# Cross-attention on one core: maxima taken from pairs of banks, two banks for scores, and two tiles in four quads of a head added up on VectorE

## The chip, the cores and the metric

The kernel runs on one core of one Trainium2 chip. The metric is the device time of one execution in microseconds (us). A core has five engines that work side by side, each through its own queue in order: TensorE (PE in the profile; its weight loads are PEld), VectorE (DVE), ScalarE (ACT), GpSimd (POOL) and SyncE (SP), which here issues the DMAs. TensorE writes its results to PSUM, eight banks of 128 partitions by 512 fp32 numbers; VectorE and ScalarE read them from there.

## What is computed

A block of three layers on x of 512 tokens by 512, with a context of 8192 tokens by 384. The change touches the first, a cross-attention with 16 heads of width 32:

```python
q = (x @ Wq + bq).reshape(B, N, NUM_HEADS, HEAD_DIM)
k = (y @ Wk + bk).reshape(B, M, NUM_HEADS, HEAD_DIM)
v = (y @ Wv + bv).reshape(B, M, NUM_HEADS, HEAD_DIM)
scores = jnp.einsum('bnhd,bmhd->bhnm', q, k) * scale
attn = jax.nn.softmax(scores, axis=-1)
out = jnp.einsum('bhnm,bmhd->bnhd', attn, v).reshape(B, N, IMAGE_DIM)
h = jax.nn.relu(out @ W1 + b1)
return h @ W2 + b2
```

N is 512 queries, M 8192 keys. A local attention and a feed-forward layer with quantized weights follow; nothing in them changes.

## The kernel before

The first 343 us project keys and values (stage "project"); the attention runs from there to about 1115 us (stage "attend"); its MLP, the local attention and the feed-forward layer fill the rest.

The keys of a head are cut into 16 **quads** of 512 keys, each into four tiles of 128. The softmax takes two passes over the scores. The first pass needs the maximum of each query: with queries on the partitions, `pre_tile` (L1042) computes 128 queries by 512 keys into a bank of `pre_ps` with four matmuls of 32 columns, and VectorE's `tile_max` (L1297) reduces it to one number a query. This pass runs two quads (`AHEAD`) before the head that uses it, so it is mixed into the work of the head before. `head_max` (L1304) reduces the 16 numbers, `row` (L1066) turns them into a row of the stacked queries, and ScalarE's `copy_row` (L1231) puts it there. The second pass has keys on the partitions: `scores` (L1079) computes one tile of 128 keys by 512 queries into a bank of `s_ps`, ScalarE writes its exponential (L1261) to `prob`, which has four slots of a quad. From `prob` come `weighted` (L1092, four fp32 matmuls a quad, summed over the head in one bank) and the denominator: GpSimd adds up tiles 0 to 2 of a quad, or 0 and 1 (even quads from 2 on), over the head (`add_up`, L1435 and L1439); `add_to_denominator` (L1103) lets TensorE sum over the partitions the one or two tiles that are left, four matmuls of 128 columns a tile; `denominator` (L1119) closes the sum with GpSimd's three tiles behind quad 1 of the next head, `invert` (L1309) takes the reciprocal, `output` (L1130) and `scale_out` (L1316) write the head's result behind quad 5.

**PSUM.** Three banks hold scores (`S_BANKS`), three hold maxima tiles, the output and the row in turn (`PRE_BANKS`), one the weighted values, one the denominator. The scores of tile n are written when the exponential of the tile that had their bank is done (semaphore `p_ready`; `s_back` says how many tiles back that is: three but for a few at the end of a head and the start of the next, two for the last tile). A maxima tile waits for the reduction three turns back (`pre_read`).

**The order of TensorE** in a quad is written out by hand, and `head` follows it, with `weighted` of the quad before at the end:

```python
PE_ORDER = ((0,), 0, (1,), 1, "den", 2, (2,), 3, (3,))
```

A number in brackets is a maxima tile, a bare one a scores tile, "den" is `add_to_denominator` for the quad two before. The last head has no maxima to take for a next one; in it VectorE does GpSimd's part (`sum_tiles`, L1345 and L1349).

## Time and profile before

| | us |
|---|---|
| median of 3 runs | 1390.31 (1388.82 to 1392.01) |
| the profiled execution | 1390.34 |
| its span | 1388.6 |
| TensorE busy | 1339.1 (96%) |
| VectorE busy | 1121.1 (81%) |
| ScalarE busy | 806.0 (58%) |
| GpSimd busy | 778.2 (56%) |

The span is from the first instruction to the last on the core; the execution's own time is 1.7 us longer. Busy time is the union of an engine's instructions. Four matmuls of 32 columns each run beside each other and are shown as four rows with nearly the same start; a matmul's row of 0.4 us reaches over the start of the next group 0.22 us later, so what a group costs is read from start to start. "Idle before" in brackets is the time in which the engine did nothing ahead of a group, with what ended it.

### The profile page before, as it was taken

The numbers are of one execution on the slowest core, as the hardware profiler recorded it, in microseconds if no ns is written. First come the engines' busy times: TensorE is split into PE (matmuls) and PEld (weight loads), VectorE is DVE, ScalarE is ACT, GpSimd is POOL, SyncE is SP. The second block draws the span as 40 slices with busy tenths as digits, with TensorE's granted clock in tenths as the row PEclk, the third lists the DMA queues.
The fourth block names the chain that finished last, engine by engine and source line by source line (L and its number), as shares of the span: only waits on it lengthen the run. The fifth ranks groups of instructions, "written<-read, shape, count | busy, mean of one in ns | idle before, by whom it ended". The sixth has DMA issues, their size and how long they took to land. (4 is left out here: it accounts for less than half of the span.)

```text
span 1388.6 us, 40034 instructions
## 1 busy us (share of the span) xinstructions
PE 1339.1 (96%) x17126; PEld 706.7 (51%) x17126; DVE 1121.1 (81%) x1786; ACT 806.0 (58%) x1459; POOL 778.2 (56%) x320
## 2 busy tenths in 40 slices
PE   7999999998999999999999999999999998999998
PEld 4444444444655554555555555545554445566554
DVE  5778888887888888888888888888886854678895
ACT  4454444453777777776777777777777831254332
POOL 0321222222999988998998898899889000201121
PEclk9999999999999999999999999999999999999999
DMA  7667777786352122121212212121211030491000
GB/s 263 178 172 227 213 216 205 207 234 186 87 176 69 38 68 67 41 64 57 69 39 68 67 38 60 64 69 38 68 55 31 5 144 1 97 226 23 0 9 23
DMA packets 127800, 137.54 MB, mean 99 GB/s; under 512 B 44996, under 2 KB 108996, under 8 KB 125700
## 3 DMA queue, kind: packets, MB, share of 16 engines
q1 hardware_dynamic: 127622, 134.98, 34.4%
q8 instruction: 135, 2.21, 0.7%
q14 instruction: 43, 0.34, 0.1%
HBM read 75.70 MB, written 44.17 MB: 86 GB/s over the span
## 5 line engine op out<-in xcount | busy, mean ns | idle before, releaser
L1297 DVE TENSOR_REDUCE early<-attend_banks 128x1 f32<-128x512 f32 x952 | 612.2, 685 | 80.8 <-PE attend_banks L1042 75.6
L1261 ACT ACTIVATE attend_prob<-attend_banks 128x512 f32<-128x512 f32 x1024 | 535.9, 600 | 200.5 <-PE attend_banks L1079 198.3
L1439 POOL TENSOR_TENSOR early<-early,attend_prob 128x1024 f32<-128x1024 f32 x210 | 614.0, 2924 | 37.7 <-ACT attend_prob L1261 9.6
L1079 PE MATMUL attend_banks<-early,k_first 97*32 97x512 f16 x2560 | 258.9, 382 | 3.1 <-ACT attend_prob L1261 3.1
L1042 PE MATMUL attend_banks<-k_first,early 96*32 96x512 f16 x2272 | 233.2, 382 | 1.1 <-PEq L285 1.1
L1042 PE MATMUL attend_banks<-attend_k_rest,early 96*32 96x512 f16 x1536 | 155.9, 380 | 0.0
L1079 PE MATMUL attend_banks<-early,attend_k_rest 97*32 97x512 f16 x1536 | 152.4, 380 | 2.8 <-ACT attend_prob L1261 2.8
L1103 PE MATMUL attend_banks<-attend_prob,ones 128*32 128x128 f32 x3048 | 134.0, 272 | 3.7 <-DVE attend_recip L1309 3.7
L1092 PE MATMUL attend_banks<-attend_prob,wkv_area 128*32 128x512 f32 x1024 | 134.2, 592 | 0.0
L1092 PE MATMUL attend_banks<-attend_prob,attend_vh_odd 128*32 128x512 f32 x1024 | 133.1, 592 | 0.0
L503 POOL TENSOR_TENSOR project_w_whole<-project_grid,project_qscale 128x704 f32<-128x704 f32 x24 | 33.3, 1386 | 172.9 <-DVE project_grid L636 172.9
L1103 PEld LDWEIGHTS attend_banks<-attend_prob,ones 128*32 128x32 f32 x3048 | 94.9, 110 | 55.1 <-DVE attend_recip L1309 11.1
L1079 PEld LDWEIGHTS attend_banks<-early,k_first 97*32 97x32 f16 x2560 | 77.7, 97 | 84.9 <-ACT attend_prob L1261 54.9
L1042 PEld LDWEIGHTS attend_banks<-k_first,early 96*32 96x32 f16 x2272 | 69.7, 97 | 60.1 <-issue 35.5
L555 ACT ACTIVATE project_v<-project_v_ps 128x512 f32<-128x512 f32 x64 | 38.1, 597 | 91.3 <-PE project_v_ps L771 91.3
L497 POOL TENSOR_TENSOR project_qn<-early,project_qinv 128x704 f32<-128x704 f32 x24 | 37.9, 1581 | 87.5 <-issue 50.2
L539 ACT ACTIVATE early<-project_k_ps,project_bk 128x512 f32<-128x512 f32 x64 | 44.0, 687 | 63.2 <-PE project_k_ps L752 62.4
L769 PE MATMUL project_v_ps<-project_w_hi,project_yT_hi 128*128 128x512 f16 x192 | 73.6, 383 | 4.2 <-ACT project_v L555 4.2
L1079 PEld LDWEIGHTS attend_banks<-early,attend_k_rest 97*32 97x32 f16 x1536 | 45.5, 96 | 58.7 <-ACT attend_prob L1261 45.0
L752 PE MATMUL project_k_ps<-project_yT_hi,project_w_hi 128*128 128x512 f16 x192 | 72.5, 379 | 1.9 <-ACT project_q_hi L574 1.4
L770 PE MATMUL project_v_ps<-project_w_lo,project_yT_hi 128*128 128x512 f16 x192 | 73.5, 383 | 0.0
L771 PE MATMUL project_v_ps<-project_w_hi,project_yT_lo 128*128 128x512 f16 x192 | 73.4, 382 | 0.0
(217 smaller groups left out, 1839.2 us busy)
## 6 DMA issues: line engine op xcount, KB each, us to landing
v_scratch<-project_v SPq DMA_DIRECT2D x16, 1024.0 KB, 9.0
early<-in_ctx_dram SPq DMA_DIRECT2D x16, 768.0 KB, 6.2
k_first<-k_scratch SPq DMA_DIRECT2D x36, 256.0 KB, 3.5
k_scratch<-project_k_hi SPq DMA_DIRECT2D x64, 128.0 KB, 2.9
k_scratch<-project_k_lo SPq DMA_DIRECT2D x64, 128.0 KB, 3.1
attend_vh_odd<-v_scratch SPq DMA_DIRECT2D x8, 1024.0 KB, 5.0
wkv_area<-v_scratch SPq DMA_DIRECT2D x7, 1024.0 KB, 4.8
attend_k_rest<-k_scratch SPq DMA_DIRECT2D x24, 256.0 KB, 3.4
```

What stands on the lines that cost most here:

```text
L539: nc.scalar.activation(kf[:, g % 2], k_ps[:, g % 2], ACT.Identity, bias=bk[:, g:g + 1], scale=1.0 / WSCALE).then_inc(kf_ready, 1)
L752: last = nc.tensor.matmul(k_ps[:, g % 2], (w_lo if p == 2 else w_hi)[:, 0, k, cols], (yT_lo if p == 1 else yT_hi)[:, u, k], start=(k, p) = ...
L769: nc.tensor.matmul(v_ps[:, t % 2], yT_hi[:, u, k, cols], w_hi[:, 1, k], start=k == 0, stop=False)
L770: nc.tensor.matmul(v_ps[:, t % 2], yT_hi[:, u, k, cols], w_lo[:, 1, k], start=False, stop=False)
L771: last = nc.tensor.matmul(v_ps[:, t % 2], yT_lo[:, u, k, cols], w_hi[:, 1, k], start=False, stop=k == CK - 1)
L1042: last = nc.tensor.matmul(pre_ps[c * HD:(c + 1) * HD, bank, :], q_stack[0:KROWS, h, queries], keys_at(s, part * BLK, (part + 1) * BLK)[0:K ...
L1079: last = nc.tensor.matmul(s_ps[c * HD:(c + 1) * HD, s_bank[n], :], key_rows[:, c * HD:(c + 1) * HD], q_stack[0:KROWS + 1, h, :], start=Tru ...
L1092: last = nc.tensor.matmul(pv_ps[t * HD:(t + 1) * HD, :], vh[s][:, BT * q + t, :], prob[:, q % PSLOTS, t, :], start=q == 0, stop=q == QUADS ...
L1103: last = nc.tensor.matmul(den_ps[t * HD:(t + 1) * HD, 0:P], ones[:], prob[:, q % PSLOTS, n, t * P:(t + 1) * P], start=q == 0 and n == summ ...
L1261: nc.scalar.activation(prob[:, q % PSLOTS, t, :], s_ps[:, s_bank[BT * q + t]], ACT.Exp, scale=SCALE).then_inc(p_ready, 1)
L1297: nc.vector.tensor_reduce(part_max[:, s, j, part:part + 1], pre_ps[:, bank], AX.X, ALU.max).then_inc(pre_read, 1)
L1439: nc.gpsimd.tensor_tensor(sums, sums, prob[:, q % PSLOTS, 0:n], ALU.add).then_inc(pool_summed, 1)
```

## The change

- `S_BANKS` goes from three to two, and `s_back` is two for every tile: scores n wait for the exponential of tile n-2. `PE_ORDER` stays.
- `PRE_BANKS` goes from three to four, used as two pairs of neighbouring banks. Maxima tiles 0 and 1 of a quad fill one pair, 2 and 3 the other; `pre_ready` is raised once a pair, and `pair_max` reduces both banks in one instruction (2 x 512 columns to 2 numbers). The wait of TensorE (`pre_read`) stands ahead of the first tile of a pair, for the pair two turns back. The output and the row each take a turn with the first bank of a pair; so behind either of them the pairs of the following quads change sides.
- In quads 2, 6, 10 and 14 (`TWO_AT`) of all heads but the last, `add_two` lets VectorE add the two tiles that GpSimd leaves (fp32, 128 x 512, SBUF to SBUF) into `two_tiles`. It stands in VectorE's queue between the two pairs of the next quad. TensorE's `add_to_denominator` for these quads waits for it (`two_added`) and takes four matmuls in place of eight. `add_two` waits for the four exponentials of the quad, and for TensorE to have read `two_tiles` last.
- The banks that the MLP uses early are numbered anew; there are five, as before.

The diff, without hunks that only rename:

```diff
@@ -58,8 +58,8 @@
 PSLOTS = 4
 POOL_TILES = 3
 DVE_TILES = 2
-S_BANKS = 3
-PRE_BANKS = 3
+S_BANKS = 2
+PRE_BANKS = 4
 TILE_RING = 8
 PE_ORDER = ((0,), 0, (1,), 1, "den", 2, (2,), 3, (3,))
 CH = 4
...
@@ -863,6 +863,8 @@
             sum_pool = piece([2, POOL_TILES * T])
             recip = sb("recip", [P, P])
             o_out = sb("o_out", [P, 2, P])
+            two_tiles = sb("two_tiles", [P, T])
+            two_added = sem("two_added")
             banks = ps("banks", [P, S_BANKS + PRE_BANKS + 2, T])
             s_ps = banks[:, 0:S_BANKS]
...
@@ -907,20 +909,27 @@
             OUTPUT_AT, ROW_AT = 5, QUADS - 2
+            PAIRS, ALL_PAIRS = TILES // 2, ALL_TILES // 2
             turns_of_head = []
             for q in range(QUADS):
-                turns_of_head += [(q, j) for j in range(TT)]
+                turns_of_head += [(q, 0), (q, 1)]
                 turns_of_head += ["output"] if q == OUTPUT_AT else ["row"] if q == ROW_AT else []
-            assert len(turns_of_head) % PRE_BANKS == 0
+            assert len(turns_of_head) % 2 == 0
             turn_of = {turn: n for n, turn in enumerate(turns_of_head)}
-            def tiles_until(n):
+            def bank_of(n):
+
+                return n % 2 * 2
+
+            def pairs_until(n):
                 return n + 1 if n < 0 else sum(turn not in ("output", "row") for turn in turns_of_head[:n + 1])
-
-            s_bank = [n % S_BANKS for n in range(TILES - 4)] + [0, 1, 2, 1]
-            s_back = [next(d for d in range(1, TILES) if s_bank[n - d] == s_bank[n]) for n in range(TILES)]
+            s_bank = [n % S_BANKS for n in range(TILES)]
+            s_back = [S_BANKS] * TILES
+
+
+            TWO_AT = (2, 6, 10, 14)
             def keys_at(s, lo, hi):
...
@@ -942,7 +951,7 @@
                 return DVE_TILES if q < LAST_SUMMED else 0
-            OUT_BANK = S_BANKS + turn_of["output"] % PRE_BANKS
+            OUT_BANK = S_BANKS + bank_of(turn_of["output"])
             h_bank = [b for b in range(S_BANKS, S_BANKS + PRE_BANKS) if b != OUT_BANK] + list(range(S_BANKS))
             EARLY_M = len(h_bank)
             h_bank += [PV_BANK, DEN_BANK, OUT_BANK]
...
@@ -1041,23 +1050,25 @@
                         queries = slice(j * P + c * HD, j * P + (c + 1) * HD)
                         last = nc.tensor.matmul(pre_ps[c * HD:(c + 1) * HD, bank, :], q_stack[0:KROWS, h, queries],
                                                 keys_at(s, part * BLK, (part + 1) * BLK)[0:KROWS], start=True, stop=True)
-                    last.then_inc(pre_ready, 1)
+                    if j % 2:
+                        last.then_inc(pre_ready, 1)
                 def pre(i, s, q, j):
                     h = 2 * i + s
                     s_of, part = (1 - s, q + AHEAD) if q < QUADS - AHEAD else (s, q + AHEAD - QUADS)
                     h_of = h + 1 if q < QUADS - AHEAD else h + 2
-                    n = turn_of[(q, j)]
+                    n = turn_of[(q, j // 2)]
                     if j == 0 and part % (QUADS // CH) == 0:
                         pe.wait_ge(k_in[s_of][part * CH // QUADS], 32 * (h_of // 2 + s_of))
-                    wait(pe, pre_read, TILES * h + tiles_until(n - PRE_BANKS))
-                    if n - PRE_BANKS == turn_of["output"]:
-                        wait(pe, o_scaled, h)
-                    if n - PRE_BANKS == turn_of["row"]:
-                        pe.wait_ge(row_set, h + 2)
-                    pre_tile(n % PRE_BANKS, h_of, s_of, part, j)
+                    if j % 2 == 0:
+                        wait(pe, pre_read, PAIRS * h + pairs_until(n - 2))
+                        if n - 2 == turn_of["output"]:
+                            wait(pe, o_scaled, h)
+                        if n - 2 == turn_of["row"]:
+                            pe.wait_ge(row_set, h + 2)
+                    pre_tile(bank_of(n) + j % 2, h_of, s_of, part, j)
                 def row(h, s, bank):
...
@@ -1098,10 +1109,14 @@
                     h = 2 * i + s
                     if q == 0:
                         wait(pe, recip_ready, h)
-                    for n in range(summed_tiles(h, q), BT):
+                    two = h < H - 1 and q in TWO_AT
+                    if two:
+                        pe.wait_ge(two_added, len(TWO_AT) * h + TWO_AT.index(q) + 1)
+                    for n in range(summed_tiles(h, q) + two, BT):
+                        tile = two_tiles if two else prob[:, q % PSLOTS, n]
                         for t in range(TT):
                             last = nc.tensor.matmul(den_ps[t * HD:(t + 1) * HD, 0:P], ones[:],
-                                                    prob[:, q % PSLOTS, n, t * P:(t + 1) * P],
+                                                    tile[:, t * P:(t + 1) * P],
                                                     start=q == 0 and n == summed_tiles(h, q), stop=False)
                     last.then_inc(den_added, 1)
...
@@ -1131,10 +1146,9 @@
                                                 pv_sum[:, s, t * P:(t + 1) * P], start=True, stop=True)
                     last.then_inc(o_ready, 1)
-                def tiles_read(h, n):
-
-                    tiles = TILES * h + tiles_until(n)
-                    return min(tiles, ALL_TILES) if isinstance(tiles, int) else tiles
+                def pairs_read(h, n):
+
+                    return min(PAIRS * h + pairs_until(n), ALL_PAIRS)
                 def head(i, s, first, last):
...
@@ -1160,12 +1174,12 @@
                             denominator(*before)
                         if q == OUTPUT_AT and not first:
                             n = turn_of["output"]
-                            pe.wait_ge(pre_read, tiles_read(h, n - PRE_BANKS))
-                            output(*before, n % PRE_BANKS)
+                            pe.wait_ge(pre_read, pairs_read(h, n - 2))
+                            output(*before, bank_of(n))
                         if q == ROW_AT and last >= 1:
                             n = turn_of["row"]
-                            pe.wait_ge(pre_read, tiles_read(h, n - PRE_BANKS))
-                            row(h + 1, 1 - s, n % PRE_BANKS)
+                            pe.wait_ge(pre_read, pairs_read(h, n - 2))
+                            row(h + 1, 1 - s, bank_of(n))
                 pe.wait_ge(fold_in, 16)
                 pe.wait_ge(ones_row, 16)
...
@@ -1291,15 +1305,24 @@
             @block.vector
             def _(dve):
-                def tile_max(s, part, j, tile, bank):
-
-                    dve.wait_ge(pre_ready, tile + 1)
-                    nc.vector.tensor_reduce(part_max[:, s, j, part:part + 1], pre_ps[:, bank], AX.X,
+                def pair_max(s, part, j, pair, bank):
+
+                    dve.wait_ge(pre_ready, pair + 1)
+                    nc.vector.tensor_reduce(part_max[:, s, 2 * j:2 * j + 2, part], pre_ps[:, bank:bank + 2], AX.X,
                                             ALU.max).then_inc(pre_read, 1)
+                def add_two(i, s, q):
+
+                    n = len(TWO_AT) * (2 * i + s) + TWO_AT.index(q)
+                    dve.wait_ge(p_ready, BT * (quad_no(i, s, q) + 1))
+                    if n:
+                        dve.wait_ge(den_added, quad_no(i, s, q) - 1 if q == TWO_AT[0] else quad_no(i, s, q - 4) + 1)
+                    nc.vector.tensor_tensor(two_tiles[:], prob[:, q % PSLOTS, BT - 2], prob[:, q % PSLOTS, BT - 1],
+                                            ALU.add).then_inc(two_added, 1)
+
                 def head_max(h, s):
-                    dve.wait_ge(pre_read, TILES * h - TT * AHEAD)
+                    dve.wait_ge(pre_read, PAIRS * h - TT * AHEAD // 2)
                     wait(dve, row_ready, h - 1)
                     nc.vector.tensor_reduce(neg_max[:, s], part_max[:, s], AX.X, ALU.max,
                                             negate=True).then_inc(max_ready, 1)
...
@@ -1378,9 +1401,12 @@
                             scale_out(*before, out_bank)
                         if last >= (1 if q < QUADS - AHEAD else 2):
                             s_of, part = (1 - s, q + AHEAD) if q < QUADS - AHEAD else (s, q + AHEAD - QUADS)
-                            for j in range(TT):
-                                tile_max(s_of, part, j, TILES * h + TT * q + j,
-                                         turn_of[(q, j)] % PRE_BANKS)
+                            for j in range(2):
+                                pair_max(s_of, part, j, PAIRS * h + 2 * q + j, bank_of(turn_of[(q, j)]))
+                                if j == 0 and q - 1 in TWO_AT:
+                                    add_two(i, s, q - 1)
+                        elif q - 1 in TWO_AT and last > 0:
+                            add_two(i, s, q - 1)
                         if q == QUADS - AHEAD - 1 and last >= 1:
                             head_max(h + 1, 1 - s)
                         if last == 0:

```

## Rows read from the trace of the kernel before

**Rows 1.** The page: busy times of the engines, and the exponentials.
```profile
PE 1339.1 (96%) x17126; PEld 706.7 (51%) x17126; DVE 1121.1 (81%) x1786; ACT 806.0 (58%) x1459; POOL 778.2 (56%) x320
...
L1261 ACT ACTIVATE attend_prob<-attend_banks 128x512 f32<-128x512 f32 x1024 | 535.9, 600 | 200.5 <-PE attend_banks L1079 198.3
```

**Rows 2.** Busy time by stretch (columns: us, each engine's busy us, clock, DMA), 351 to 1066.
```profile
351.00:1066.00 715.00, 708.39 (x12616) 375.60 (x12608) 622.49 (x983) 507.06 (x969) 653.03 (x222) 1.00 0.21 63
```

**Rows 3.** The waits (total us, times, longest), 351 to 1066.
```profile
ACT attend_prob L1261 <- PE attend_banks L1079: 190.5, 207, 1.4
PEld attend_banks L1079 <- ACT attend_prob L1261: 82.7, 288, 0.8
```

**Rows 4.** Order of time (start, us, engine; [idle before]), a quad with one denominator tile.
```profile
705.02 0.40 PE L1042 MATMUL attend_banks<-k_first,early 96*32 96x512 f16 x4
...
705.23 0.40 PE L1079 MATMUL attend_banks<-early,attend_k_rest 97*32 97x512 f16 x4
...
705.46 2.60 DVE L1297 TENSOR_REDUCE early<-attend_banks 128x1 f32<-128x512 f32 x4 [0.23 <-PE attend_banks L1042]
...
705.76 2.07 ACT L1261 ACTIVATE attend_prob<-attend_banks 128x512 f32<-128x512 f32 x4 [0.95 <-PE attend_banks L1079]
...
705.89 0.40 PE L1103 MATMUL attend_banks<-attend_prob,ones 128*32 128x128 f32 x8
...
706.11 0.40 PE L1079 MATMUL attend_banks<-early,attend_k_rest 97*32 97x512 f16 x4
...
706.40 0.10 PEld L1079 LDWEIGHTS attend_banks<-early,attend_k_rest 97*32 97x32 f16 x4 [0.18 <-ACT attend_prob L1261]
...
706.55 0.40 PE L1079 MATMUL attend_banks<-early,attend_k_rest 97*32 97x512 f16 x4
...
708.06 0.40 PE L1079 MATMUL attend_banks<-early,attend_k_rest 97*32 97x512 f16 x4
```

**Rows 5.** Order of time, maxima 3 of quad 5 and maxima 0 of quad 6.
```profile
700.67 0.40 PE L1042 MATMUL attend_banks<-k_first,early 96*32 96x512 f16 x4
...
701.97 0.40 PE L1042 MATMUL attend_banks<-k_first,early 96*32 96x512 f16 x4
```

**Rows 6.** Order of time, scores and exponentials of the last quad of a head.
```profile
728.93 0.59 PE L1079 MATMUL attend_banks<-early,attend_k_rest 97*32 97x512 f16 x4
...
729.73 1.58 ACT L1261 ACTIVATE attend_prob<-attend_banks 128x512 f32<-128x512 f32 x3
...
730.87 0.40 PE L1079 MATMUL attend_banks<-early,attend_k_rest 97*32 97x512 f16 x4 [0.26 <-ACT attend_prob L1261]
...
732.39 0.39 PE L1079 MATMUL attend_banks<-early,k_first 97*32 97x512 f16 x4
```

**Rows 7.** The reciprocals of 397 to 738.9 us, and scores 0 and 3 of one quad 2.
```profile
L1309 DVE RECIPROCAL attend_recip<-attend_banks x7: 957/958/959, 397.5 to 690.1; 128x128 f32<-128x128 f32 x7
...
397.51 0.39 PE L1079 MATMUL attend_banks<-early,k_first 97*32 97x512 f16 x4
...
399.24 0.40 PE L1079 MATMUL attend_banks<-early,k_first 97*32 97x512 f16 x4
```

**Rows 8.** VectorE: groups by line, order of time, and line 1349 (ns min/median/max).
```profile
L616 DVE TENSOR_REDUCE project_amax<-early 128x44 f32<-128x704 f32 x24 | 21.1, 878 | 0.2 <-DMA early<-in_L_ffn_w_gate_dram 0.2
...
725.75 0.22 DVE L1304 TENSOR_REDUCE early<-early 128x4 f16<-128x64 f32 x1
...
L1349 DVE TENSOR_TENSOR early<-early,attend_prob x12: 1214/1220/1227, 1079.6 to 1106.4; 128x1024 f32<-128x1024 f32 x12
```

**Rows 9.** Order of time, scores 0 and 1 of two quads of the last head.
```profile
1083.28 0.60 PE L1079 MATMUL attend_banks<-early,attend_k_rest 97*32 97x512 f16 x8
...
1085.54 0.60 PE L1079 MATMUL attend_banks<-early,attend_k_rest 97*32 97x512 f16 x8
```

**Rows 10.** Busy time by stretch, after the attention (columns as in rows 2).
```profile
1162.00:1166.00 4.00, 2.67 (x23) 2.24 (x21) 2.48 (x7) 0.98 (x2) 0.00 (x0) 1.00 0.00 0
1166.00:1170.00 4.00, 2.05 (x10) 1.12 (x11) 2.30 (x4) 1.30 (x3) 0.00 (x0) 0.88 0.02 4
```

More of the change, by code:

```diff
@@ L1200, in _ @@
                 pe.wait_ge(o_scaled, H - 1)
-                output(LASTPAIR, 1, turn_of["output"] % PRE_BANKS)
+                output(LASTPAIR, 1, bank_of(turn_of["output"]))
                 hidden(1, range(DK - 1))
@@ L1265, in head @@
                         if q == ROW_AT and last >= 1:
-                            copy_row(h + 1, turn_of["row"] % PRE_BANKS)
+                            copy_row(h + 1, bank_of(turn_of["row"]))
                         if last == 0 and q in O_HIGH_AT:
@@ L1331, in split_weights @@
                                                    op0=ALU.mult, op1=ALU.subtract).then_inc(mlp_split, 1)
-                out_bank = turn_of["output"] % PRE_BANKS
+                out_bank = bank_of(turn_of["output"])
                 SPLIT_AT = (2, 4, 5, 7, 8, 10)
```

## The prediction

> **What bounds the kernel now.** I read the page first. TensorE is busy 96% of the span, VectorE 81%, ScalarE and GpSimd under 60% [rows 1]. Two thirds of the span are the attention of 16 heads, so I took the busy times of 351 to 1066 us, where 15 heads with maxima for the next head run: TensorE shows 708.4 of 715 us at a granted clock of 1.00, VectorE 622, GpSimd 653, ScalarE 507 [rows 2]. Matmul busy time overlaps itself, so I checked it against the order of time. A head is 16 quads, and a quad of TensorE is: maxima tile 0, scores 0, maxima 1, scores 1, sum of the denominator, scores 2, maxima 2, scores 3, maxima 3, weighted values. Groups of four follow each other every 0.22 us without a gap: maxima 0 at 705.02, scores 0 at 705.23, the denominator at 705.89, scores 2 at 706.11, and after maxima 2 scores 3 at 706.55 [rows 4]. A quad with one denominator tile takes 2.83 us (scores 0 at 705.23, the next at 708.06), one with two 3.05 us (maxima 0 at 701.97 to 705.02) [rows 4, 5]. TensorE bounds these heads by its order of work alone; ScalarE waits for it 190.5 us [rows 3]. The other wait in the list speaks of how near ScalarE is: weight loads of scores wait for ScalarE 82.7 us, 288 times [rows 3]. That wait costs nothing now, because it ends before the array is free: the load of scores 3 is let go at 706.40, its matmul has its turn at 706.55 [rows 4]. This is the place that the change touches.
>
> **Part 1, scores get two banks instead of three.** Scores n may be written when the exponential of tile n-3 is done now, of tile n-2 after; with that, scores 3 waits for exponential 1, and scores 2 for exponential 0. The chain is all in rows. Scores 0 starts at 705.23, its exponential at 705.76: 0.53. From that start to the release of a waiting load: 706.40 - 705.76 = 0.64 to 0.65. Exponentials follow each other every 0.49 us ((1.58 - 0.60) / 2) [rows 1, 4, 6]. So scores 2 can start 0.53 + 0.64 = 1.17 us after scores 0, and scores 3 at 0.53 + 0.49 + 0.64 = 1.66; take 1.65. Today scores 2 starts 0.88 after scores 0 (706.11) and scores 3 1.32 (706.55) in a quad with one denominator tile, 0.22 more in one with two. There is one place where the kernel of before has just this wait: in the last quad of each head scores 3 has the bank of scores 1. There the exponentials start at 729.73, so the second at 730.22, and scores 3 starts at 730.87, 0.65 later, weight load and matmul together, after an idle array [rows 6]. So nothing else is in the release, and nothing hides it: TensorE's queue is in order, and behind the wait stand maxima 2, maxima 3 and the weighted values. From scores 3 to the next scores 0 it is 708.06 - 706.55 = 1.51 as now, 0.01 more after an idle array. New quad: 1.65 + 1.52 = 3.17 us, whether it has one denominator tile or two.
> Per head: 7 quads with one tile (the odd ones but the last) +0.34 each = 2.4; 7 with two (0, 4, 6, ... 14) +0.12 each = 0.8. Quad 2 waits already for the reciprocal between scores 1 and 2: 397.51 to 399.24 = 1.73 from scores 0 to 3 [rows 7], over 1.65, so +0.0. Quad 15 pays its wait already, with an exponential that starts late behind the copy of the row of maxima: 3.46 us (728.93 to 732.39) [rows 6]; new 3.17, so -0.3. Sum 2.9 us.
>
> **Part 2, maxima in pairs.** A reduction of 704 columns takes 0.88 us, one of 64 columns 0.22: 1.03 ns for a column, so one over two banks 0.88 + 0.33 = 1.21 us; the upper bound is two single ones, 2.60 / 2 = 1.30 [rows 4, 8]. I take 1.20, since one instruction pays its start once. VectorE then has 2.4 us in a quad instead of 2.6. It wasn't the bound (its row has 0.23 of idle ended by TensorE [rows 4]), so this gains nothing. What it costs: a pair of banks comes free only when both tiles are read, and the next pair but one needs it. In a plain quad that is a whole quad later, with 0.6 us or more to spare. After the output (behind quad 5) and after the row (behind quad 14) the pairs change sides: maxima 0 of the next quad need the pair that maxima 2 and 3 of this quad wrote. From maxima 3 to the next maxima 0 it is 701.97 - 700.67 = 1.30 us now [rows 5], with output or row in between (0.22 each). New: reduction 0.44 after the matmuls (705.02 to 705.46 [rows 4]), 1.20 long, 0.05 for the release (an exponential's 0.65 less its 0.60): 1.69. So +0.39 twice a head, 0.8 us. The bounds are 0 (the read is hidden) and 0.5 (1.30 long). The bank of the output or the row itself is wanted by the second pair of the next quad, some 1.6 us after its first, time enough for one scaling or copy.
> By the Trainium skill, Perfetto Trace Analysis, section Optimizing Scalar/DVE Operations, grouping helps an engine that is saturated, and an engine that isn't but makes bubbles on another should have its instructions broken up. By the first half the pairs would free 0.2 us a quad; the trace shows VectorE waiting for TensorE (0.23 [rows 4]), so the second half is the one that applies here, with these 0.8 us.
>
> **Part 3, VectorE adds two tiles in four quads.** Sums of 128x1024 take 1.22 us here; with 512 columns less at 1.03 ns it is 0.69 [rows 8]. Four of them stand between the pairs of quads 3, 7, 11 and 15, which then hold 2.4 + 0.69 = 3.1 us of VectorE in 3.17, and the second pair ends 0.1 or 0.2 us late, with 0.6 to spare. VectorE waits there for exponential 3 of the quad before, which has ended before pair 0 of this quad is read. Behind it is queued only pair 1. TensorE wants the sum in the denominator step one quad later. On TensorE it takes away 16 matmuls in four of the quads with two tiles: 0.22 us each (705.89 to 706.11 [rows 4]), 60 quads in all, 13.2 us. But the step stands between scores 1 and scores 2, and scores 2 then waits for exponential 0: it would start at 1.17 with or without it. So the gain on the path is nil; the 13.2 us turn into waiting. Bounds: -13.2 (no such wait) and 0.
>
> **The last head** has no maxima; its quads take 1085.54 - 1083.28 = 2.26 us [rows 9]: by the chain above scores 3 starts 1.17 after scores 0 already, so 1.09 is left to the next scores 0. New: 1.65 + 1.09 = 2.74, 16 x 0.48 = +7.7 us. The MLP behind it has five early banks, as before: nothing.
>
> **Sum.** 15 x (2.9 + 0.8) = 55.5, less 0.4 for head 0, which has no output: 55.1; with 7.7 it is 63 us. On the profiled execution's 1390.34 us (span 1388.6, the median of the runs 1390.31, the same) that is 1453. As a check of the counting: 7 reciprocals mark six heads from 397.5 to 690.1, 48.77 us each [rows 7]; my quads of before (7 x 2.83, 7 x 3.05, 3.24, 3.46) with output, row and the closing sum of three denominator tiles (0.22 + 0.22 + 0.66) make 49.0.
>
> **Rivals.**
> Scores are not held back (not slower, or faster): if exponential 0 lets go of its bank within 0.88 us of scores 0, the third bank was spare, the 13.2 us of part 3 count in full and part 2 costs 11 at most: 1388, or 1377 if the read of a pair also hides. It decides below 0.88; the rows have 1.17 at each scores 3, and the last quads a real idle array. 4 in 100.
> The wait is longer than a release: a matmul after an idle array starts later by its weight load (0.10, the load at 706.40 [rows 4]). Then +0.1 in each of 256 quads, 1480; against it stands the start at 730.87 of load and matmul together. Half of it, 1467, is in my range. 6 in 100 for beyond 1474.
> VectorE becomes the bound: if the add next to GpSimd's sums takes twice as long (1.4), quads 3, 7, 11, 15 hold 3.8 us of VectorE against 3.17, and 0.6 of lateness meets 0.6 of spare. It would have to last longer still; at +0.5 in each of 60 quads, 1484. GpSimd, busy 653 of 715 us now [rows 2], gets 8% more time for the same sums. 2 in 100.
> TensorE's clock falls. It is at 2.4 GHz all through the heads, and stretches with gaps keep it (2.67 busy us of 4 at 1.00), while after one with 2.05 of 4 at 0.88 it has fallen [rows 10]. The new heads work 2.82 us of 3.17, the last one 2.2 of 2.74. Were it to fall, nearly each 0.22 would be 0.44: +2 us in 256 quads, 1900. 1 in 100. The Trainium skill (TensorE: Matmul & The Clock Gate, Part 1) has the same two states, set by how busy the array has been; by its rule the clock stays as well.
>
> **Numbers.** My forecast, slower by 3.5 to 6%, holds 87 in 100: the chain is pinned to some 0.05 us a quad (13 us), and pairs to 0.1 us at two places. Range 1438 to 1474. A measurement of this kernel can tell some 0.2%, 2.8 us, from no change. Faster by more 0.03, within 0.02, slower 0.95.
>
> **What would show it.** Quads of 3.17 us from scores 0 to scores 0, alike with one and with two denominator tiles; TensorE idle in front of scores 2 and scores 3, ended by the exponential; reductions of 1024 columns at 1.2 us; 2808 denominator matmuls instead of 3048 with no time to show for it; idle of 0.4 us in front of maxima 0 of quads 6 and 15, ended by VectorE. Quads of 2.9 us, or scores 2 starting 0.9 us after scores 0, would make the forecast wrong.

## The result, and the profile after

The changed kernel takes 1462.61 us (median of 4 runs, 1461.80 to 1464.76) against 1390.84 us for the kernel before: a ratio of 1.0519, 95% interval 1.0506 to 1.0532. It is 71.8 us slower. The forecast was 1453 us (1438 to 1474), 63 us slower.

| | before | after |
|---|---|---|
| median | 1390.84 | 1462.61 |
| span of the profiled execution | 1388.6 | 1461.5 |
| TensorE busy | 1339.1 | 1378.0 |
| VectorE busy | 1121.1 | 1122.6 |
| ScalarE busy | 806.0 | 827.0 |

The busy time of the stretch in which 15 heads take maxima for the next, 351 to 1130 us, answers to [rows 2]. The columns are those of [rows 2].

```profile
351.00:1130.00 779.00, 744.37 (x12136) 298.92 (x12132) 623.51 (x571) 524.91 (x967) 653.65 (x221) 1.00 0.20 58
```

TensorE is idle 35 us of 779 here, against 7 of 715, at the same granted clock of 1.00 (2.4 GHz). VectorE and GpSimd are busy for the same time as before (623.5 and 653.7 us, against 622.5 and 653.0) in a longer stretch. The waits of this stretch answer to [rows 3]:

```profile
ACT attend_prob L1275 <- PE attend_banks L1090: 232.4, 221, 1.7
PEld attend_banks L1090 <- ACT attend_prob L1275: 217.3, 633, 0.7
DVE early L1311 <- PE attend_banks L1051: 150.7, 382, 1.0
POOL early L1465 <- ACT attend_prob L1275: 69.8, 103, 1.3
```

The wait of the scores' weight loads (L1090 is L1079 of before) for ScalarE has grown from 82.7 us, 288 times, to 217.3 us, 633 times. ScalarE and VectorE wait more for TensorE, too: all of them stand in the one loop of scores, exponential and bank, and each of them has gaps in it. In order of time, one quad (it answers to [rows 4]):

```profile
702.85 0.39 PE L1090 MATMUL attend_banks<-early,k_first 97*32 97x512 f16 x4
...
703.37 2.19 ACT L1275 ACTIVATE attend_prob<-attend_banks 128x512 f32<-128x512 f32 x4 [0.99 <-PE attend_banks L1090]
703.50 0.39 PE L1118 MATMUL attend_banks<-attend_two_tiles,ones 128*32 128x128 f32 x8
703.51 1.23 DVE L1311 TENSOR_REDUCE early<-attend_banks 128x2 f32<-128x1024 f32 x1 [0.23 <-PE attend_banks L1051]
704.02 0.10 PEld L1090 LDWEIGHTS attend_banks<-early,k_first 97*32 97x32 f16 x4 [0.40 <-ACT attend_prob L1275]
704.02 0.40 PE L1090 MATMUL attend_banks<-early,k_first 97*32 97x512 f16 x4
...
704.51 0.40 PE L1090 MATMUL attend_banks<-early,k_first 97*32 97x512 f16 x4
...
706.03 0.39 PE L1090 MATMUL attend_banks<-early,k_first 97*32 97x512 f16 x4
```

Scores 0 start at 702.85, scores 2 at 704.02, scores 3 at 704.51, the next scores 0 at 706.03. That is 1.17, 1.66 and 3.18 us after scores 0; the forecast had 1.17, 1.65 and 3.17. Weight load and matmul of scores 2 start together at 704.02, 0.65 after the exponential of 703.37. The following quad, with an ordinary denominator tile, takes 3.19 (706.03 to the scores 0 of 709.22). Behind the row of maxima the new stall of the pairs is seen:

```profile
711.11 0.39 PE L1051 MATMUL attend_banks<-k_first,early 96*32 96x512 f16 x4
...
711.55 1.23 DVE L1311 TENSOR_REDUCE early<-attend_banks 128x2 f32<-128x1024 f32 x1 [0.45 <-PE attend_banks L1051]
...
712.83 0.40 PE L1051 MATMUL attend_banks<-k_first,early 96*32 96x512 f16 x4 [0.25 <-DVE early L1311]
```

Maxima 3 at 711.11, maxima 0 of the next quad at 712.83: 1.72 us, ended by the reduction over both banks. Behind the output it is 1.81 (416.32 to 418.13 in the trace) in place of 1.30 [rows 5]. Behind the row the kernel before did not take 1.30, as the prediction had assumed, but 1.09:

```profile
727.61 0.39 PE L1042 MATMUL attend_banks<-k_first,early 96*32 96x512 f16 x4
...
728.70 0.40 PE L1042 MATMUL attend_banks<-k_first,early 96*32 96x512 f16 x3
```

So the new stall is 0.51 us behind the output and 0.63 behind the row.

### The profile page after: what moved, and what is told of

Same layout as the page of the kernel before. It is cut to its first block and busy times, and to the rows that moved or that the text cites. A ratio compares the mean times of both kernels' runs of the same rounds, so it can differ in the third digit from the quotient of the medians.

```text
span 1461.5 us, 38717 instructions
## 1 busy us (share of the span) xinstructions
PE 1378.0 (94%) x16646; PEld 625.3 (43%) x16646; DVE 1122.6 (77%) x1370; ACT 827.0 (57%) x1459; POOL 779.5 (53%) x320
## 5 line engine op out<-in xcount | busy, mean ns | idle before, releaser
L1311 DVE TENSOR_REDUCE early<-attend_banks 128x2 f32<-128x1024 f32 x476 | 582.5, 1224 | 156.2 <-PE attend_banks L1051 155.4
L1275 ACT ACTIVATE attend_prob<-attend_banks 128x512 f32<-128x512 f32 x1024 | 556.4, 595 | 250.4 <-PE attend_banks L1090 244.6
L1090 PE MATMUL attend_banks<-early,k_first 97*32 97x512 f16 x2560 | 253.3, 387 | 16.6 <-ACT attend_prob L1275 1.6
L1051 PE MATMUL attend_banks<-k_first,early 96*32 96x512 f16 x2272 | 223.7, 383 | 7.0 <-DVE early L1311 5.9
L1090 PE MATMUL attend_banks<-early,attend_k_rest 97*32 97x512 f16 x1536 | 149.6, 384 | 11.1 <-ACT attend_prob L1275 0.8
L1051 PE MATMUL attend_banks<-attend_k_rest,early 96*32 96x512 f16 x1536 | 150.1, 380 | 3.0 <-DVE early L1311 3.0
L1090 PEld LDWEIGHTS attend_banks<-early,k_first 97*32 97x32 f16 x2560 | 67.8, 95 | 170.0 <-ACT attend_prob L1275 147.3
L1118 PE MATMUL attend_banks<-attend_prob,ones 128*32 128x128 f32 x2088 | 92.0, 272 | 3.7 <-DVE attend_recip L1332 3.7
L1051 PEld LDWEIGHTS attend_banks<-k_first,early 96*32 96x32 f16 x2272 | 61.4, 96 | 62.3 <-issue 40.6
L1090 PEld LDWEIGHTS attend_banks<-early,attend_k_rest 97*32 97x32 f16 x1536 | 40.3, 95 | 107.0 <-ACT attend_prob L1275 97.8
L1118 PEld LDWEIGHTS attend_banks<-attend_prob,ones 128*32 128x32 f32 x2088 | 60.6, 110 | 49.1 <-DVE attend_recip L1332 11.2
L1461 POOL TENSOR_TENSOR early<-attend_prob 128x1536 f32<-128x1536 f32 x15 | 51.9, 3461 | 52.6 <-issue 37.9
```

What stands on the lines that cost most here:

```text
L1051: last = nc.tensor.matmul(pre_ps[c * HD:(c + 1) * HD, bank, :], q_stack[0:KROWS, h, queries], keys_at(s, part * BLK, (part + 1) * BLK)[0:K ...
L1090: last = nc.tensor.matmul(s_ps[c * HD:(c + 1) * HD, s_bank[n], :], key_rows[:, c * HD:(c + 1) * HD], q_stack[0:KROWS + 1, h, :], start=Tru ...
L1118: last = nc.tensor.matmul(den_ps[t * HD:(t + 1) * HD, 0:P], ones[:], tile[:, t * P:(t + 1) * P], start=q == 0 and n == summed_tiles(h, q), ...
L1275: nc.scalar.activation(prob[:, q % PSLOTS, t, :], s_ps[:, s_bank[BT * q + t]], ACT.Exp, scale=SCALE).then_inc(p_ready, 1)
L1311: nc.vector.tensor_reduce(part_max[:, s, 2 * j:2 * j + 2, part], pre_ps[:, bank:bank + 2], AX.X, ALU.max).then_inc(pre_read, 1)
L1461: nc.gpsimd.tensor_tensor(sums, prob[:, 0, 0:n], prob[:, 1, 0:n], ALU.add).then_inc(pool_summed, 2)
```

## Experiments

All times are medians; the kernel before was timed beside each. Line numbers in rows are those of each kernel.

**Undoing the change part by part.** First, two banks for scores without the pairs and without the adds. Edit of the kernel before:

```diff
-            s_bank = [n % S_BANKS for n in range(TILES - 4)] + [0, 1, 2, 1]
-            s_back = [next(d for d in range(1, TILES) if s_bank[n - d] == s_bank[n]) for n in range(TILES)]
+            s_bank = [n % 2 for n in range(TILES)]
+            s_back = [2] * TILES
```

> The kernel before with one edit: scores use two of their three banks, so that scores n wait for exponential n-2. Maxima are still taken one tile at a time from three banks, and VectorE adds nothing. Theory (the wait for the exponential carries the loss): quads of 3.18 us in place of 2.83 and 3.05, no stall behind output and row; the head grows by the 4.34 us seen with the whole change less the two stalls behind output and row (0.51 and 0.42), 3.4 us, times 15 is 51, and 7.7 in the last head: 1450 us. Rival (the pairs of banks carry it): 1391 to 1395 us, quads stay at 2.83 and 3.05.

Measured: 1449.1 us (ratio 1.0422, 1.0406 to 1.0437), 58.3 us slower. The wait alone carries four fifths of the loss, and the rival falls.

Second, the changed kernel without its adds:

```diff
-            TWO_AT = (2, 6, 10, 14)
+            TWO_AT = ()
```

> The changed kernel without its third part: no adds on VectorE, TensorE takes eight matmuls in quads 2, 6, 10 and 14 again. Theory (those matmuls lie within the wait for exponential 0): the same quads of 3.18 us, 1462 to 1463 us, no difference. Rival (the adds give their 13.2 us also here, and the loss of the rest is 85 us): 1476 us.

Measured: 1462.70 us against 1462.61 with the adds (ratios to before 1.0507, 1.0487 to 1.0527, and 1.0519). The 240 matmuls that the adds remove are worth nothing here. A quad with two denominator tiles shows why:

```profile
703.43 0.39 PE L1090 MATMUL attend_banks<-early,k_first 97*32 97x512 f16 x4
...
704.09 0.61 PE L1118 MATMUL attend_banks<-attend_prob,ones 128*32 128x128 f32 x16
704.60 0.40 PE L1090 MATMUL attend_banks<-early,k_first 97*32 97x512 f16 x4
```

These are scores 0, the denominator with 16 matmul rows where the quad above has 8, and scores 2. Scores 2 again start 1.17 us after scores 0. So the loss splits into 58.3 us for the two banks, 13.6 for the pairs (1462.7 - 1449.1), and 0 for the adds, which the intervals know to some 3 us.

**The adds alone, on the kernel before.** This tests what the 240 matmuls are worth where no wait covers them. Main edits (the rest is `two_tiles` and its waits as in the change):

```diff
+            TWO_AT = (2, 6, 10, 14)
...
                                 tile_max(s_of, part, j, TILES * h + TT * q + j,
                                          turn_of[(q, j)] % PRE_BANKS)
+                                if j == 1 and q - 1 in TWO_AT:
+                                    add_two(i, s, q - 1)
```

> The kernel before with one part of the change alone: VectorE adds two tiles in quads 2, 6, 10 and 14, TensorE takes four matmuls there in place of eight; three banks for scores, three for single maxima tiles. The add stands behind maxima tile 1 of the next quad. Theory (TensorE is the bound in the kernel before, and the 240 matmuls are on its path as long as no wait covers them): 60 x 0.22 = 13.2 us less, 1378 us. Rival 1 (VectorE, with 2.6 + 0.6 us in a quad of 2.83, makes TensorE wait for maxima banks): 0.3 us back in each of 60 quads, 1396 us. Rival 2 (GpSimd, 5.85 us for two quads that get 5.66, becomes the bound through the four slots of prob): no gain, 1390 us.

Measured: 1408.95 us, ratio 1.0130 (1.0115 to 1.0146): slower than before by 18 us, where my theory had 13 faster. None of the three had it so. The row of the adds, and two of them in order of time with GpSimd's sums about them (line 1461):

```profile
L1315 DVE TENSOR_TENSOR attend_two_tiles<-attend_prob x60: 679/1712/1993, 353.7 to 1088.0; 128x512 f32<-128x512 f32 x60
...
590.88 1.72 DVE L1315 TENSOR_TENSOR attend_two_tiles<-attend_prob 128x512 f32<-128x512 f32 x1
...
592.19 3.73 POOL L1461 TENSOR_TENSOR early<-early,attend_prob 128x1536 f32<-128x1536 f32 x1
...
604.02 0.68 DVE L1315 TENSOR_TENSOR attend_two_tiles<-attend_prob 128x512 f32<-128x512 f32 x1
...
604.77 3.47 POOL L1461 TENSOR_TENSOR early<-early,attend_prob 128x1536 f32<-128x1536 f32 x1 [0.69 <-ACT attend_prob L1269]
...
PEld attend_banks L1046 <- DVE early L1305: 57.2, 115, 1.3
PE attend_banks L1046 <- DVE early L1305: 17.2, 27, 0.8
```

The first row has the least, middle and greatest duration in ns: 679, 1712, 1993. The add at 604.02 falls into a gap of GpSimd and takes 0.68 us. The one at 590.88 starts while a sum of GpSimd runs (it ends at 592.05); the add ends at 592.60, 0.4 us after the next sum has begun, and that sum takes 3.73 us in place of 3.47. VectorE then is late with its reductions, and TensorE waits for maxima banks (the last two rows, of 420 to 1060 us: 57.2 us of the weight loads, of which a part is idle that these loads have in any case, and 17.2 us of the matmuls; of before the same wait has 0.3 us in 351 to 1066). The Trainium skill (SBUF — State Buffer, section SBUF: two separate sides) says that a VectorE instruction with two SBUF inputs and a GpSimd instruction that reads SBUF shut each other out for a whole instruction. The trace agrees as far as it goes: the add of 590.88 ends 0.55 us after the sum it met, and alone it takes 0.68. The reductions read PSUM; beside GpSimd's sums they take the 0.68 us (median of 952) that they take with GpSimd nearly idle in the runs below.

To see whether it is GpSimd, or VectorE being too full in any case, two kernels with GpSimd's sums cut to 8 of 512 columns, so that the softmax denominators lack the rest:

```diff
-                        nc.gpsimd.tensor_tensor(sums, sums, prob[:, q % PSLOTS, 0:n],
+                        nc.gpsimd.tensor_tensor(sums[:, :, 0:8], sums[:, :, 0:8], prob[:, q % PSLOTS, 0:n, 0:8],
```

> The kernel before with VectorE's adds alone, and GpSimd's sums cut to 8 of 512 columns a tile, so the softmax denominators lack those sums; all waits stay. Theory (an add of VectorE from SBUF takes 0.68 us alone and 1.7 us beside a sum of GpSimd): all 60 adds take 0.68 us, VectorE keeps up, and the 13.2 us of the removed matmuls arrive: 1378 us. Rival (VectorE is too full for the adds in any case, 2.6 + 0.6 us in a quad of 2.83): 1400 us or more.

> The kernel before with GpSimd's sums cut in the same way and nothing else (the softmax denominators lack them): the base for the run above. TensorE is the bound, so 1390 us, within 0.2%. If GpSimd held the kernel before back through the slots of prob, it would be faster, by up to 10 us.

Measured: with the adds 1377.43 us (ratio 0.9893, 0.9870 to 0.9916), without them 1391.21 (1.0006, 0.9995 to 1.0016).

```profile
L1315 DVE TENSOR_TENSOR attend_two_tiles<-attend_prob x60: 679/681/693, 353.7 to 1057.0; 128x512 f32<-128x512 f32 x60
```

With GpSimd out of the way all 60 adds take 0.68 us, and the 13.2 us of the matmuls arrive (13.8 between the two). So the matmuls are worth their time, VectorE has room for the adds, and the collision takes it away. GpSimd's own length holds nothing back in the kernel before.

**Another order for two banks.** If the loss is the wait for an exponential, it should go when scores stand further apart. First try, with the weighted values halved by key tiles:

```diff
-PE_ORDER = ((0,), 0, (1,), 1, "den", 2, (2,), 3, (3,))
+PE_ORDER = (0, (0,), (1,), 1, "den", (2,), 2, (3,), "w0", 3, "w1")
...
+                            elif step in ("w0", "w1"):
+                                half = range(0, 2) if step == "w0" else range(2, BT)
```

> The changed kernel with another hand-written order of TensorE and nothing else: scores 0, maxima 0, maxima 1, scores 1, denominator, maxima 2, scores 2, maxima 3, first two matmuls groups of the weighted values, scores 3, the last two. Scores 0 to 2 are then 1.3 us apart and 1 to 3 1.5 us, over the 1.18 and 1.17 that a bank takes to come free, and maxima 3 stand 1.74 us ahead of the next maxima 0 where output or row lie between. Theory (two banks cost only what the order leaves uncovered): quads of 2.83 us again (3.05 in three of 16), head 47.3 us against 48.8 before, last head 0.2 us a quad over before: 1371 us, below both kernels. Rival 1 (two banks can't feed ScalarE in any order): over 1450 us. Rival 2 (GpSimd, 5.85 us for two quads, is the next bound): quads of 2.93, some 1393 us.

Measured: 1438.84 us (1.0345, 1.0330 to 1.0361). Better than the changed kernel by 24 us, far from 1371. My cut was bad: a key tile's weighted matmul uses 32 of the 128 columns of the array, and four run side by side. With half of them, two of the four matmuls of scores 3 start beside the half at 718.26, and the other two only in the group at 719.12:

```profile
718.26 0.60 PE L1103 MATMUL attend_banks<-attend_prob,attend_vh_odd 128*32 128x512 f32 x2
718.26 0.39 PE L1090 MATMUL attend_banks<-early,attend_k_rest 97*32 97x512 f16 x2
718.49 1.03 PE L1103 MATMUL attend_banks<-attend_prob,attend_vh_odd 128*32 128x512 f32 x6
719.12 0.62 PE L1090 MATMUL attend_banks<-early,attend_k_rest 97*32 97x512 f16 x6
719.55 0.62 PE L1051 MATMUL attend_banks<-k_first,early 96*32 96x512 f16 x8
719.56 2.36 ACT L1278 ACTIVATE attend_prob<-attend_banks 128x512 f32<-128x512 f32 x4 [0.70 <-PE attend_banks L1090]
720.21 0.10 PEld L1090 LDWEIGHTS attend_banks<-early,attend_k_rest 97*32 97x32 f16 x4 [0.54 <-ACT attend_prob L1278]
720.21 0.40 PE L1090 MATMUL attend_banks<-early,attend_k_rest 97*32 97x512 f16 x4
```

The array time is not what this costs: from the first half to the next maxima 0 it is 1.29 us here (718.26 to 719.55), and 1.30 in the second try below (706.13 to 707.43 in its trace). What it costs is that scores 3 are complete late. Their exponential starts at 719.56, 1.30 us after their first matmuls, against 0.45 in the second try (706.56 to 707.01). The next scores 1 need its bank and start 0.65 after it, at 720.21, 0.22 us later than their turn: 0.66 behind maxima 0, where the second try has 0.44 (707.43 to 707.87). These 0.22 us are the difference between quads of 3.05 (maxima 0 at 716.50 and 719.55) and of 2.83. So the wait for an exponential was still there, in front of another tile.

Second try, the same order with the weighted values halved by queries, so that each half uses all the columns of the array for half the time; with the adds and without:

```diff
+                        parts = [slice(half * T // 2, (half + 1) * T // 2) for half in halves]
+                    for cols in parts:
...
+                            last = nc.tensor.matmul(pv_ps[t * HD:(t + 1) * HD, cols], vh[s][:, BT * q + t, :],
+                                                    prob[:, q % PSLOTS, t, cols],
```

> The same without the adds of VectorE. Theory: quads of 2.83 (nine) and 3.05 (seven), head 48.4 us against 48.8 before since the wait in the last quad is gone too, last head 3.4 us longer in all: 1388 us. Rival (two banks hold TensorE back in any order): over 1440 us.

> The changed kernel with the order scores 0, maxima 0, maxima 1, scores 1, denominator, maxima 2, scores 2, maxima 3, weighted (columns 0 to 255), scores 3, weighted (columns 256 to 511). The weighted values are now halved by queries and not by key tiles, so each half takes 0.43 us; only those of the first and last quad of a head stay whole, at the end. Theory (two banks cost only what the order leaves uncovered): no idle of TensorE in front of scores, quads near 2.83 us. The adds of VectorE then meet GpSimd's sums more often: if each takes 1.7 us as in the run with the adds alone, VectorE needs 4 x 2.45 + 1.7 = 11.5 us in four quads of 11.5, and the gain of 13.2 us is partly given back: 1375 to 1400 us. Without any collision 1375. Rival (two banks hold TensorE back in any order): over 1440 us.

Measured without the adds: 1396.47 us (1.0038, 1.0025 to 1.0051). The order alone takes 66 of the 72 us back with two banks for scores and pairs for maxima. Scores 0 of three quads, and the wait for ScalarE (420 to 1050 us):

```profile
704.38 0.40 PE L1090 MATMUL attend_banks<-early,attend_k_rest 97*32 97x512 f16 x4
...
707.21 0.40 PE L1090 MATMUL attend_banks<-early,attend_k_rest 97*32 97x512 f16 x4
...
710.26 0.40 PE L1090 MATMUL attend_banks<-early,attend_k_rest 97*32 97x512 f16 x4
...
PEld attend_banks L1090 <- ACT attend_prob L1284: 15.8, 54, 0.4
```

2.83 and 3.05 us, as in the kernel before. It misses my 1388 by 8 us. They lie in the heads, which take 48.95 us on average (heads 1 to 13) where I had 48.4; quad 1, for one, takes 3.70 against 3.48 of before. What holds it there I did not take apart.

Measured with the adds: 1417.62 us (1.0190, 1.0171 to 1.0208), 21 us worse than without, and 21 us better than the first try, which has the adds too. The adds take 1355 ns in the middle (679 to 1710), and the waits for reductions are 30.6 us of TensorE's weight loads and 19.8 of its matmuls (420 to 1050 us). The cost of the collision was underrated again. My reading, which no run tests by itself, is that VectorE's load over four quads counts less than that it is late for single banks.

**Two edits that follow.** One add a head, at the gap of GpSimd, on the kernel before:

```diff
+            TWO_AT = (2,)
```

> The kernel before with VectorE's add in quad 2 alone of each head (of four in the run with adds only). There GpSimd has a gap of 0.7 us when the add runs, and it took 0.68 us. Theory (what made the adds lose is their overlap with GpSimd's sums): 15 x 0.22 = 3.3 us gained and nothing given back, 1387.7 us on a base of 1391. Rival (each add costs VectorE's lateness wherever it stands): 1391 to 1396 us.

Measured: 1389.17 us (0.9983, 0.9974 to 0.9992), 1.7 us less, half of what was expected. The adds take 682 ns in the middle, one of them 1779.

And the wait that I had used as evidence, in the last quad of each head, taken out (ScalarE reads by the same count):

```diff
-                    wait(pe, p_ready, BT * quad_no(i, s, 0) + n + 1 - s_back[n])
+                    wait(pe, p_ready, BT * quad_no(i, s, 0) + n + 1 - S_BANKS)
...
-                        last = nc.tensor.matmul(s_ps[c * HD:(c + 1) * HD, s_bank[n], :], key_rows[:, c * HD:(c + 1) * HD],
+                        last = nc.tensor.matmul(s_ps[c * HD:(c + 1) * HD, (TILES * h + n) % S_BANKS, :], key_rows[:, c * HD:(c + 1) * HD],
```

> The kernel before with the three banks of scores counted on over the heads, so that every tile, the last of a head too, waits for the exponential three tiles back. Theory (the wait for exponential 1 in the last quad, of the kind that the change made everywhere, costs 0.5 us a head: scores 3 start at 730.87, and would start when exponential 0 releases, 729.73 + 0.64 = 730.37): 15 x 0.5 = 7.5 us less, 1383.5 us. Rival (the wait is covered by what follows): 1391 us.

Measured: 1383.41 us (0.9944, 0.9932 to 0.9957), 7.5 us less, as forecast. The last quad of a head, from its scores 0 to the next:

```profile
726.59 0.59 PE L1077 MATMUL attend_banks<-early,attend_k_rest 97*32 97x512 f16 x4
...
729.56 0.44 PE L1077 MATMUL attend_banks<-early,k_first 97*32 97x512 f16 x4
```

2.97 us against 3.46 [rows 6].

> Both edits: banks counted on over the heads, one add a head in quad 2. Theory: both terms stand beside each other, 7.5 + 3.3 = 10.8 us less, 1380 us, below both kernels. Rival: the add meets GpSimd's sum again because the heads are shorter, then 1383 us or more.

Measured for both: 1382.76 us (0.9931, 0.9917 to 0.9944), 2.8 us over my 1380. Over the banks alone it is 0.65 us less, too little for the intervals to tell; 14 of the 15 adds take 0.68 us and the first 1.16, so the rival's reason, adds that meet sums again, is not seen either.

## Why the prediction was right, and by how much its terms were off

**The wait of the scores** was the cause, at the place and of the size that the rows of before gave. The quad is 3.18 or 3.19 us against 3.17. The one place with an idle array, in the last quad of a head [rows 6], was the row that decided, since it showed that load and matmul start together 0.65 us after the exponential; the rival of a longer release (1480) fell with it. Two banks alone are 58.3 us in the run with nothing else, where the forecast had 15 x 2.9 and 7.7, 51.2.

**The pairs** cost 13.6 us between two runs, where the forecast had 15 x 0.8 less 0.4, 11.6. The reduction takes 1.23 us where I took 1.20.

**The adds** are worth nothing in this kernel, as forecast: the time with and without is the same. They take 0.68 us as forecast (0.69).

**The sum was 9 us short**, and the term that was too small is the head's 3.7 us: it measured 4.34. The reciprocals are (776.7 - 404.9) / 7 = 53.11 us apart against 48.77 [rows 7]:

```profile
L1332 DVE RECIPROCAL attend_recip<-attend_banks x8: 958/958/958, 404.9 to 776.7; 128x128 f32<-128x128 f32 x8
```

Where it lies is seen quad by quad, from scores 0 to scores 0 (us, medians of heads 1 to 13; the head is the mean):

| quads | before | two banks alone | after |
|---|---|---|---|
| 3, 7, 9, 11, 13 | 2.83 | 3.19 | 3.19 |
| 0, 4, 6, 8, 10, 12 | 3.05 | 3.19 | 3.19 |
| 1, closing sum | 3.48 | 3.84 | 3.84 |
| 2, reciprocal | 3.24 | 3.24 | 3.24 |
| 5, output | 3.05 | 3.40 | 3.92 |
| 14, row | 3.08 | 3.21 | 3.84 |
| 15 | 3.47 | 3.47 | 3.19 |
| head | 48.77 | 52.25 | 53.12 |

- Growths of 0.36 and 0.14 where the forecast had 0.34 and 0.12 make 0.3 us a head.
- The stall behind the output is 0.51 us for 0.39, and behind the row 0.63: together 0.4 us. The forecast gave the row a turn of 0.22 us of TensorE in the kernel before; it takes 0.01 there (1.09 us to maxima 0, where a quad with nothing between has 1.08, 706.76 to 707.84). That is also why the prediction's own check came to 49.0 us where the head took 48.77, a difference that I let stand as small, and that times 15 is 3 us.
- Quad 15 loses 0.3 us, as forecast, but not by the two banks. With them alone it stays at 3.47, because its exponential 0 starts late behind the copy of the row (759.10, scores 2 at 759.75, for scores 0 at 758.29). The pairs take it away: with the stall ahead of its maxima 0 the copy is done sooner.

```profile
758.48 0.59 ACT L1231 ACTIVATE early<-attend_banks 1x512 f16<-1x512 f32 x1 [0.69 <-PE attend_banks L1066]
...
759.10 2.19 ACT L1261 ACTIVATE attend_prob<-attend_banks 128x512 f32<-128x512 f32 x4
...
759.75 0.40 PE L1079 MATMUL attend_banks<-early,attend_k_rest 97*32 97x512 f16 x4 [0.21 <-ACT attend_prob L1261]
```

**Head 0** was to be 0.4 us cheaper than the others, since it has no output. That was wrong: its pairs change sides all the same, and from maxima 3 of quad 5 to the next maxima 0 it is 1.81 us there, too (363.25 to 365.06), where a plain quad has 1.08. It grew by 6.2 us (47.56 to 53.76) for a forecast of 3.3. Some 1.5 us of this stand in its quad 1, 4.64 us long, at the lower clock (below).

**The last head** has quads of 2.75 us (scores 0 at 1160.79 and 1163.54), forecast 2.74. Yet from its first scores 0 to those of its last quad it grew by 5.9 us, and not by 15 x 0.48 = 7.2: in the kernel before its quads 9, 11 and 13 took 2.55 us, and quad 2 takes 3.03 before and 3.02 after. So an error of the other sign hides a part of what the heads were short, which is luck, too.

**The rivals.** "Scores are not held back" was priced at 1377 to 1388, with the 13.2 us of the adds "in full". That price was wrong, though the rival's chance was not tested by it: where scores are not held back, with the new order, the adds cost 21 us, and on the kernel before 18. I had priced the adds beside GpSimd at 1.4 us and as a rival of 2 in 100 in the changed kernel. In that kernel no add is held up (60 of 680 to 693 ns), since its longer quads leave GpSimd idle where the add runs. Its waits for ScalarE in the sums of line 1465 are 69.8 us, 103 times; the sum next to an add:

```profile
569.09 0.68 DVE L1320 TENSOR_TENSOR attend_two_tiles<-attend_prob 128x512 f32<-128x512 f32 x1
...
569.58 3.51 POOL L1465 TENSOR_TENSOR early<-early,attend_prob 128x1536 f32<-128x1536 f32 x1 [1.04 <-ACT attend_prob L1275]
```

The sum starts 0.19 us before the add ends, and takes 3.51 us for 3.47. So the 0.69 of my working, taken from adds of a head in which GpSimd has no sums, was met because the wait of the first part had made room. That is luck in this term; the add's price in the kernel before shows it.

The clock stayed at 1.00 in the heads from 351 us on, as its rival's row said. At the entry of the attention, which no row of the prediction covers, it is at its lower level (0.50, 1.2 GHz) in both kernels, in the one before until some time in 345 to 347 us (0.63 there), in the changed one until about 351. The kernel before and then the changed one, 347 to 349 us:

```profile
347.00:349.00 2.00, 2.00 (x36) 0.80 (x28) 2.00 (x4) 1.90 (x4) 0.17 (x1) 1.00 1.01 232
...
347.00:349.00 2.00, 2.00 (x27) 0.47 (x16) 1.86 (x2) 1.06 (x3) 0.00 (x0) 0.50 1.02 266
```

The profile of the run with the banks counted on, where the quads are those of before, has 0.50 in this stretch as well, so it is not shown that the change makes it. The price of this rival does not add up either: 2 us in 256 quads on top of 1453 are 1965 us, not 1900.

## What to carry to other kernels

Before a bank is taken from a ring, measure the loop from writing it to its release (here 1.17 us) and compare it with the spacing of its writers in the engine's order; what is missing is paid on each turn, and work removed inside the gap is worth nothing. The loop counts from the last part of the bank to be written, as the first try of the other order showed. A sum by heads should be checked against the measured head quad by quad, until nothing is left over. With the spacing changed in place of the banks, 66 of 72 us came back. A duration of a VectorE add with both inputs in SBUF holds only for what GpSimd does in that moment, so look at what GpSimd runs in the rows that the duration is from.

## What was new about the hardware

- VectorE's add of 128x512 from SBUF takes 0.68 us beside an idle GpSimd and up to 1.99 us beside its sums in the run with the adds alone; GpSimd's sum of 128x1536 grows from 3.47 to 3.73 us. Reductions from PSUM are not touched (0.68 us either way).
- Half of a group of four fp32 matmuls of 32 columns leaves room for half of a group of scores beside it. Halving the weighted values by key tiles took no more array time than halving by queries (1.29 and 1.30 us to the next maxima 0), but the scores between the halves were complete later (exponential 1.30 us after their first matmuls, against 0.45), which made quads of 3.05 us for 2.83.
- The row of maxima (four matmuls of one column) takes no turn of its own in the kernel before: 1.09 us from maxima 3 to the next maxima 0 with it, 1.08 without, 1.30 with the output.
- One reduction over two PSUM banks (1024 columns) takes 1.23 us, two single ones 1.29: 0.06 us less a pair in the time to the last result.
